# A six-stage decoder kernel: loads of a group split by reader, and the last norms written to the second state buffer

## The reference

```
x = LN(x + retention(x))               # 8 heads of 16, decay mask, group norm, gate
x = LN(x + cross_attention(ctx, x))    # 8 heads of 16, masked softmax over 64 context tokens
x = LN(x + moe(x))                     # 8 experts, top 2, rerouted by a similarity matrix
x = LN(x + attention(x))               # 16 heads of 64, scores outside a band of 129 set to 0
x = LN(x + attention_with_context(x))  # 16 heads of 8, 64 context tokens put before the 64 own
x = LN(x + block(x))                   # rotary attention, LN, 8 experts of 512 (gelu), top 2, LN
```

## Time and profile before

| | us |
|---|---|
| median of the runs | 2297.73 |
| the profiled execution | 2298.89 |
| its span | 2297.3 |
| PE busy (85%) | 1944.6 |
| DVE busy (54%) | 1234.6 |
| ACT busy (38%) | 875.9 |
| POOL busy (16%) | 376.7 |
| PE idle until the last of the six loads landed | 44.5, at 8 places |
| PE idle until a reloaded `X` landed | 15.6, at 3 places |

### The profile page before, as it was taken

How to read it: one execution, slowest core, us unless ns; L and a number is a source line. 1 busy time by engine, 2 the same in 40 slices (tenths; PEclk the granted TensorE clock), 3 DMA queues, 4 the chain that set the end, 5 groups by cost and what they waited for, 6 DMA issues and landing times.

```text
span 2297.3 us, 41641 instructions
## 1 busy us (share of the span) xinstructions
PE 1944.6 (85%) x17716; PEld 1380.0 (60%) x17716; DVE 1234.6 (54%) x3227; ACT 875.9 (38%) x1472; POOL 376.7 (16%) x370
## 2 busy tenths in 40 slices
PE   4867767678888899988898998988989989888996
PEld 3645555554556676655666665565766655566764
DVE  5657565647556533466656235656643457565331
ACT  1212122112456353335554433355443333553532
POOL 5132322300201101012111011111011021011011
PEclk8777777769899799999988999999889999997999
DMA  4010101010000012100000121000002210000121
GB/s 168 6 51 1 56 1 56 1 37 1 11 1 11 1 38 65 47 19 11 11 1 1 56 65 45 3 11 11 2 19 61 59 29 11 1 11 1 38 61 41
DMA packets 82201, 64.21 MB, mean 28 GB/s; under 512 B 15960, under 2 KB 69216, under 8 KB 81760
## 3 DMA queue, kind: packets, MB, share of 16 engines
q1 hardware_dynamic: 82016, 61.56, 9.0%
HBM read 57.35 MB, written 4.19 MB: 27 GB/s over the span
## 4 chain that ended last, share of the span: by engine, by line
PE 60%; DVE 21%; ACT 7%; POOL 6%; issue 3%; DMA 2%; SPq 1%; POOLq 0%; DVEq 0%
PE bank L1636 10%; PE bank L1627 9%; PE bank L1413 4%; DVE P L1080 4%; DVE gs L1079 4%; PE bank L1525 4%; PE bank L1250 3%; PE bank L1588 3%; PE bank L1421 3%; DVE X L893 2%; PE bank L1493 2%; PE bank L1438 2%; PE bank L1576 2%; PE bank L1265 2%; PE bank L1536 2%
## 5 line engine op out<-in xcount | busy, mean ns | idle before, releaser
L1068 DVE SCALAR_TENSOR_TENSOR R<-bank,gs,R 128x128 f32<-128x128 f32 x480 | 134.5, 343 | 297.2 <-PE bank L1636 251.8
L861 ACT ACTIVATE PT<-bank,cols 128x512 f32<-128x512 f32 x256 | 174.4, 686 | 298.1 <-PE bank L1627 297.7
L1636 PEld LDWEIGHTS bank<-w2r,PT 128*128 128x128 f32 x2048 | 236.3, 192 | 49.3 <-ACT PT L861 39.9
L1636 PE MATMUL bank<-w2r,PT 128*128 128x128 f32 x2048 | 246.1, 277 | 21.7 <-ACT PT L861 21.7
L763 ACT ACTIVATE P<-P 128x512 f32<-128x512 f32 x256 | 159.2, 629 | 250.5 <-DVE P L1080 249.1
L1627 PE MATMUL bank<-XT,w1r 128*128 128x512 f32 x512 | 242.5, 609 | 3.1 <-DVE R L1209 3.1
L1079 DVE TENSOR_REDUCE gs<-bank 128x8 f32<-128x512 f32 (+1 forms) x256 | 174.5, 682 | 96.1 <-PE bank L1525 66.3
L1250 PE MATMUL bank<-const,P 128*128 128x128 f32 x1152 | 181.8, 298 | 33.1 <-POOL P L652 14.5
L1250 PEld LDWEIGHTS bank<-const,P 128*128 128x128 f32 x1152 | 143.9, 152 | 93.8 <-ACT P L763 36.8
L594 POOL TENSOR_SCALAR rstd<-mv 128x4 f32<-128x4 f32 x64 | 14.7, 230 | 1126.8 <-DVE mv L885 1126.8
L1080 DVE TENSOR_TENSOR P<-bank,gs 128x512 f32<-128x512 f32 x256 | 176.9, 691 | 8.8
(11 more groups left out here) (205 smaller groups left out, 3245.0 us busy)
## 6 DMA issues: line engine op xcount, KB each, us to landing
w1r<-in_w SPq DMA_DIRECT2D x64, 256.0 KB, 2.7
w2r<-in_w SPq DMA_DIRECT2D x64, 256.0 KB, 3.1
wb<-in_wb SPq DMA_DIRECT2D x1, 4228.0 KB, 17.4
V<-in_ctxT SPq DMA_DIRECT2D x16, 256.0 KB, 3.7
XT<-in_xT SPq DMA_DIRECT2D x8, 256.0 KB, 2.9
X<-in_x SPq DMA_DIRECT2D x8, 256.0 KB, 4.1
V<-in_mask SPq DMA_DIRECT2D x8, 256.0 KB, 4.2
x_mid<-X SPq DMA_DIRECT2D x8, 256.0 KB, 2.3
```

The lines of the kernel that those rows point to most:

```text
L861: act.activation(PT[s][:, c, :], banks[s][c % 3][:, :], ACT.Gelu, bias=Col("b1", NC * e + c)).then_inc(b_gelu.of(s), 1)
L1068: last = dve.scalar_tensor_tensor(R[s][:, t, :], bank[:, 128 * t:128 * t + 128], share[s][:, t, e:e + 1], src[:, t, :], ALU.mult, ALU.add)
L1636: ins = mm(tile(banks[s][3], t), tile(PT[s][:, c, :], t), w2r[e % 2][:, c, :], start=c == 0, stop=c == NC - 1)
```

## The change

The six loads of a group are split into three parts with a semaphore each: `XT` (`xT_loaded`, PE waits at `qk`), context and masks (`ctx_loaded`, waited for at `kv` by PE and at `qk.3` by POOL), and `X` (`x_loaded`, waited for by DVE at `o`). Each is issued for the slot's next group when its buffer has had its last reader in this one: context and masks after `q`, `X` after its transpose and POOL's copy with the bias, `XT` after the gate logits. PE's `qk` now also waits for `a_g_done` of the slot's group before.

The last norm of each phase is written to `X1` in place of `X`, and stored from there. So the load of the next `X` needs no wait for a store; in phase 2 it is issued as soon as POOL 687 has read `X` (`b_r2`). POOL waits for the store before it writes `X1` again, much later in the next group. At the start of the program `X` is loaded after the masks. Many signals of phase 2 now go on counting on a semaphore of phase 1, which adds no instruction.

All tables in `ORDERS` but `pool1` have new numbers.

```diff
 ORDERS = dict(
-    sp1=(0, 1, 1, 1, 2, 1, 3, 1, 4, 1, 5, 1, 6, 1, 7, 1),
+    sp1=(0, 2, 1, 2, 0, 2, 1, 2, 2, 2, 3, 2, 2, 2, 3, 2, 4, 2, 5, 2, 4, 2, 5, 2, 6, 1, 7, 1),
...
-    pe2=(0, 1, 1, 1, 0, 1, 1, 1, 0, 1, 1, 1, 0, 1, 1, 1, 0, 2, 1, 2, 0, 1, 1, 1, 0, 3, 1, 3, 0, 3, 1, 3, 0, 3, 1, 3,
...
             def second(n, s, last):
+                if not last:
+                    yield "q"
+
+                    sp.wait_ge(a_q.of(s), a_q.at(n, s))
+                    load_context(n + 1, s)
+                    yield "o2"
+                    sp.wait_ge(a_x_ps.of(s), a_x_ps.at(n, s, use=0))
+                    sp.wait_ge(a_x_bias.of(s), a_x_bias.at(n, s))
+                    load_x(n + 1, s)
+                    yield "g"
+                    sp.wait_ge(a_g_ps.of(s), a_g_ps.at(n, s))
+                    load_xT(n + 1, s)
                 yield "gb"
                 sp.wait_ge(a_x.of(s), a_x.at(n, s, use=1))
-                apart(sp)
-                sp.dma_start(token_rows(x_mid, n, s), X[s][:, :, :]).then_inc(stored[s], 16)
-                if not last:
-
-                    sp.wait_ge(a_g_done.of(s), a_g_done.at(n, s))
-                    apart(sp)
-                    sp.wait_ge(stored[s], 16 * n + 16)
-                    apart(sp)
-                    loads(n + 1, s)
+                sp.dma_start(token_rows(x_mid, n, s), X1[s][:, :, :]).then_inc(stored[s], 16)
...
+                if not last:
+                    yield "n5s"
+
+                    sp.wait_ge(b_r2.of(s), b_r2.at(n, s))
+                    load_state(n + 1, s)
                 yield "n5"
                 sp.wait_ge(b_x.of(s), b_x.at(n, s, use=3))
-                apart(sp)
-                sp.dma_start(token_rows(out, n, s), X[s][:, :, :]).then_inc(written[s], 16)
-                if not last:
-                    sp.wait_ge(written[s], 16 * n + 16)
-                    apart(sp)
-                    load_state(n + 1, s)
+                sp.dma_start(token_rows(out, n, s), X1[s][:, :, :]).then_inc(written[s], 16)
...
                 yield "on"
-                norm_apply(n, s, a_ln_rstd, a_x, 1)
+                norm_apply(n, s, a_ln_rstd, a_x, 1, X1[s])
...
                 yield "n5"
-                norm_apply(n, s, b_ln_rstd, b_x, 5)
+                norm_apply(n, s, b_ln_rstd, b_x, 5, X1[s])
...
-                pe.wait_ge(loaded[s], 16 * 6 * (n + 1))
+                if n:
+                    pe.wait_ge(a_g_done.of(s), a_g_done.at(n - 1, s))
+                pe.wait_ge(xT_loaded[s], 16 * (n + 1))
...
                 yield "kv"
                 pe.wait_ge(a_x.of(s), a_x.at(n, s))
+                pe.wait_ge(ctx_loaded[s], 16 * 4 * (n + 1))
```

More of the change, by code:

```diff
@@ L82, in then @@
     def then(self, passes, each=1, uses=1):
-        assert len(self.sems) == SLOTS
-        return Signal(self.sems, each, uses, self.at(passes - 1, 0, use=self.uses - 1))
+        return Signal(self.sems, each, uses, self.at(passes - 1, SLOTS - 1, use=self.uses - 1))
 class Steps:
@@ L333, in build @@
         s_const2 = sem("s_const2")
-        loaded = [sem(f"loaded{s}") for s in range(SLOTS)]
+        xT_loaded = [sem(f"xT_loaded{s}") for s in range(SLOTS)]
+        x_loaded = [sem(f"x_loaded{s}") for s in range(SLOTS)]
+        ctx_loaded = [sem(f"ctx_loaded{s}") for s in range(SLOTS)]
         stored = [sem(f"stored{s}") for s in range(SLOTS)]
-        a_qk_ps = signal("a_qk_ps", 4)
-        a_qk_mul = signal("a_qk_mul", 4)
+        a_qk_ps = signal("qk_ps", 4)
+        a_qk_mul = signal("qk_mul", 4)
         a_k_sum = signal("a_k_sum", 3)
@@ L342, in build @@
         a_v_diag = signal("a_v_diag")
-        a_tanh = signal("a_tanh")
+        a_tanh = signal("tanh")
         a_gated = signal("a_gated")
@@ L356, in build @@
         a_hT = signal("a_hT")
-        a_o_ps = signal("a_o_ps")
+        a_o_ps = own("o_ps", 1, 2)
         a_ln_mv = own("ln_mv", 1, 2)
@@ L372, in build @@
         a_pT = own("pT", 4)
-        a_r_ps = signal("a_r_ps", 4)
-        a_r = signal("a_r")
+        a_r_ps = own("r_ps", 4)
+        a_r = own("r")
         a_rt_ps = own("rt_ps")
         a_rT = own("rT")
-        a_o2_ps = signal("a_o2_ps")
-        a_g_ps = signal("a_g_ps")
+        a_g_ps = signal("g_ps")
         a_g_diff = own("g_diff", 1)
         a_g_exp = own("g_exp", 1)
-        a_g_done = signal("a_g_done")
+        a_g_done = signal("g_done")
         a_x_bias = own("x_bias", 1)
-        a_spread = signal("a_spread")
+        a_spread = signal("spread")
         dve1, pool1 = Steps(sem("dve1")), Steps(sem("pool1"))
@@ L420, in build @@
         b_up_ps = own("b_up_ps", 2, 8)
-        b_tanh = own("b_tanh", 1, 8)
+        b_tanh = a_tanh.then(passes, 1, 8)
         b_fh = own("b_fh", 1, 8)
@@ L447, in build @@
         b_pT = a_pT.then(passes, 4, 8)
-        b_r_ps = own("b_r_ps", 1, 6)
-        b_r = own("b_r", 1, 6)
+        b_r_ps = a_r_ps.then(passes, 1, 6)
+        b_r = a_r.then(passes, 1, 6)
         b_rt_ps = a_rt_ps.then(passes, 1, 2)
         b_rT = a_rT.then(passes, 1, 2)
-        b_o_ps = own("b_o_ps", 1, 2)
-        b_fqk_ps = signal("b_fqk_ps", 4)
-        b_frot = signal("b_frot", 4)
+        b_o_ps = a_o_ps.then(passes, 1, 2)
+        b_fqk_ps = a_qk_ps.then(passes, 4, 1)
+        b_frot = a_qk_mul.then(passes, 4, 1)
         b_fsum = signal("b_fsum", 2)
@@ L459, in build @@
         b_fv = signal("b_fv")
-        b_g_ps = signal("b_g_ps")
+        b_g_ps = a_g_ps.then(passes)
         b_g_diff = a_g_diff.then(passes)
         b_g_exp = a_g_exp.then(passes)
-        b_g_done = signal("b_g_done")
+        b_g_done = a_g_done.then(passes)
         b_b2_ps = signal("b_b2_ps")
@@ L466, in build @@
         b_x_bias = a_x_bias.then(passes, 1, 3)
-        b_spread = signal("b_spread")
+        b_spread = a_spread.then(passes)
         b_tspread = signal("b_tspread", 1, 4)
@@ L490, in token_rows, with load_xT, load_x, load_context @@
                 return dram[bass.ds((n * SLOTS + s) * NT, NT), :].rearrange("(t p) d -> p t d", p=128)
-            def loads(n, s):
+            def load_xT(n, s):
                 t0 = (n * SLOTS + s) * NT
-                sp.dma_start(XT[s][:, :], d["xT"][:, bass.ds(t0, NT)]).then_inc(loaded[s], 16)
+                sp.dma_start(XT[s][:, :], d["xT"][:, bass.ds(t0, NT)]).then_inc(xT_loaded[s], 16)
+            def load_x(n, s):
+                sp.dma_start(X[s][:, :, :], token_rows(d["x"], n, s)).then_inc(x_loaded[s], 16)
+            def load_context(n, s):
+                t0 = (n * SLOTS + s) * NT
                 for c in range(2):
                     sp.dma_start(ctxT[s][:, c, :], d["ctxT"][c * 128:c * 128 + 128, bass.ds(t0, NT)])\
-                      .then_inc(loaded[s], 16)
-                sp.dma_start(X[s][:, :, :], token_rows(d["x"], n, s)).then_inc(loaded[s], 16)
+                      .then_inc(ctx_loaded[s], 16)
                 sp.dma_start(maskr[s], d["mask"][bass.ds(t0, NT)].partition_broadcast(128))\
-                  .then_inc(loaded[s], 16)
+                  .then_inc(ctx_loaded[s], 16)
                 sp.dma_start(maskc[s][:, :], d["mask"][bass.ds(t0, NT)].rearrange("(t p) -> p t", p=128),
-                             allow_slow_non_contiguous=True).then_inc(loaded[s], 16)
+                             allow_slow_non_contiguous=True).then_inc(ctx_loaded[s], 16)
+            def loads(n, s):
+                load_xT(n, s)
+                load_context(n, s)
+                load_x(n, s)
             def first(n, s):
@@ L627, in second @@
                 yield "q"
+                if n:
+                    pool.wait_ge(stored[s], 16 * n)
                 with_bias(n, s, a_x, a_x_bias, "xbo")
@@ L645, in first2 @@
                 yield "aq0"
+                if n:
+                    pool.wait_ge(written[s], 16 * n)
                 with_bias(n, s, b_x, b_x_bias, "abo", 0)
@@ L979, in first @@
                 dve.wait_ge(a_o_ps.of(s), a_o_ps.at(n, s))
+                dve.wait_ge(x_loaded[s], 16 * (n + 1))
                 st1(dve.tensor_tensor(R[s][:, :, :], tok(banks[s][2][:, :]), X[s][:, :, :], ALU.add))
@@ L1024, in second @@
                 yield "o2"
[L1025 removed]
+                dve.wait_ge(a_o_ps.of(s), a_o_ps.at(n, s, use=1))
                 dve.wait_ge(a_x_bias.of(s), a_x_bias.at(n, s))
@@ L1360, in second @@
                     ins = mm(o, tile(OT[s], t), tile(A("xo"), 1), start=False, stop=True)
-                ins.then_inc(a_o2_ps.of(s), 1)
+                ins.then_inc(a_o_ps.of(s), 1)
                 yield "x"
                 pe.wait_ge(a_x.of(s), a_x.at(n, s, use=1))
-                turn_state(s, 3, X, a_x_ps)
+                turn_state(s, 3, X1, a_x_ps)
                 yield "g"
```

23 lines of the change are left out of this document (14 added, 9 removed), and 176 rows, old and new, of tables (act1, act2, dve1, dve2).

## The result

The changed kernel takes 2177.18 us, median of 4 runs (2176.25 to 2178.56); the kernel before, run beside it, 2292.18. The ratio is 0.950, 95% interval 0.944 to 0.956. The profiled execution took 2176.25 us with a span of 2174.5. The one of before had 2297.3, so the span fell by 122.8 us. The medians differ by 115.0, since the execution profiled before (2298.89) was 6.7 us above the median.

What follows compares the result with a forecast made beforehand. It took phase 1 to be bound by chains from engine to engine and phase 2 nearly by PE. Its terms summed to 61.5 us less than the profiled 2298.89, forecast 2237 us, range 2202 to 2276.

Steps and rivals of the forecast that it cites:

- The clock: PE's granted clock around phase 1's `qk` stalls: claimed the stall alone didn't lower it, so nothing was counted.
- Rival 1: Clock comes back in phase 1's six `qk`, 19 us less than forecast: 2218 us; chance 13%.
- The six stalls and the start: PE's waits for loads at `qk` in phase 1 go, -28.5 us; waits at program start shorten, -5 us.
- Rival 2: Phase 1 stays bound by its chains, the time returns in other waits, none of 28.5 gained: 2265.5 us; chance 15%.
- Softmax order of phase 1: Slot 1's score tiles come ahead of slot 0's products on PE, so DVE idles less: 2 us four times, -8.
- The reload: Phase 2's reload of `X` for slot 1 is issued earlier, with PE work placed there: 3 x 5.2, -15.6 us.
- Rival 3: Phase 2 gives nothing at its seams: reload idle turns into waits for POOL, start is even: 2260.6 us; chance 15%.
- The start of phase 2: Slot 1's experts fill PE's idle time in layer 4; slot 0's seven alone lose 3 us: -8 us taken.
- `fv`: PE's waits for values of layer 6's attention, 22.3 us at eight places, covered by the other slot's stages: -18 us.
- `cs` behind `cr`: PE's waits for DVE's output tile come at three places a pass, not one: 8 more at 2.7, +21.6 us.
- rival 5: Slower through POOL's scaled tiles in phase 2, 89.5 us more waiting: 2326 us; decides from 4.75 us a round; chance 5%.

Runs made afterwards that it cites:

- E5: Kernel before, with three unread extra products on PE ahead of `qk`'s wait for the six loads, groups 2 to 7: 2268.40 us, ratio 0.993.
- E1: Changed kernel with all engines' order tables taken from the kernel before, keeping the new loads: 2248.96 us, ratio 0.981.
- E9: Changed kernel with slot 0's first scores of layer 6 moved back directly behind its `fv` on PE, all four passes: 2205.16 us, ratio 0.965.
- E3: Changed kernel with phase 2's order tables taken from the kernel before; loads and phase 1 stay new: 2222.83 us, ratio 0.969.

## Why the prediction was wrong, by its own steps

1. **The clock** is the step that failed. "So the stall alone didn't bring it down, and my sum leaves the clock as it is": the first half holds, the second does not follow. I asked what had lowered the clock and not what kept it low. Busy time fell by 48.7 us, of which the six stalls are 20 (E5: 19.4; E1: 21.7). Rival 1 had that mechanism and I gave it 13%. Its 19 us agree with these 20 partly by luck: it had all six `qk` at 6.40 us falling to 3.2, but they gave 11.4 in the kernel after (36.9 to 25.5 us) and 14.7 in E5, and the rest came behind them. It was also too narrow, since busy time fell in other places too: 7.9 us more with phase 1's orders, and 19.1, give or take 10, in phase 2. The Trainium skill's rule, "TensorE: Matmul & The Clock Gate", section "Why this matters for your kernels", that idle gaps between bursts of matmuls make the throughput drop in mid-kernel, is borne out by E9, where the clock falls from 1.00 behind a wait of 3.9 us. E5 shows something else that a gap does: the clock was low ahead of it, and filling it brought the clock back. I had set the rule aside on one row.
2. *The six stalls and the start*, 33.5: right in sum, 32.6 of idle time (E1). `qk` began at 8.10 rather than 13.09, and what it waits for there is POOL's memset, not `XT`. The second wait at the start did not go, as I had said it would: slot 1's `qk` waited 4.16 us for its `XT` (2.87 before). Rival 2 fell. A pass of phase 1 takes 99 us where I said 107: the 12 us of idle time came as forecast (35.2 to 23.3), and 8.4 of busy time (84.1 to 75.7) came on top.
3. *Softmax order of phase 1*, 8: all of phase 1's new orders together give 9.1 of idle time, and 7.9 of busy time that I had not counted. DVE's waits for score tiles fell from 4.1 us a pass to 0.5; no run takes these apart from the rest.
4. *The reload*, 15.6: right in mechanism; the loads alone give nothing in the passes (E3), the order makes them count. Rival 3 therefore fell only because both were changed.
5. *The start of phase 2*, 8: wrong, though the time seems to fit. From the first `sh` to the first store of the output it takes 397.83 us after and 405.46 in E3, 7.6 less. But only 3.3 of these are idle time (46.9 to 43.6), the rest is clock, and PE's waits for `fv`'s values, 5.5 us of that idle time, belong to the next term. So nothing is left for the start. The loss was mis-sized: slot 0's experts alone wait 1.27 us seven times (8.9 where I had 3). My chain of 3.05 us from product to `down` was nearly right (438.15 to 441.31, 3.16), but I set PE's `down` of 1.05 against it, and that stands ahead of the chain, not in it. So an expert takes 4.15 us from `down` to `down`.

```profile
437.16 1.16 PE L1443 MATMUL bank<-wb,P 128*128 128x128 f32 x8 [1.27 <-DVE P L1116]
438.15 1.88 PE L1435 MATMUL bank<-XT,wb 128*128 128x512 f32 x4
441.31 1.16 PE L1443 MATMUL bank<-wb,P 128*128 128x128 f32 x8 [1.27 <-DVE P L1116]
```

6. *`fv`*, 18: 22.3 of waiting, the whole. E9 shows 29 us for 15.4 of it.
7. *`cs` behind `cr`*, +21.6: wrong. The waits for DVE rose by 6.3 (10.7 to 17.0), to 3.0 once and 0.7 twice a pass. That DVE has less queued at the two others may be the reason; no run tells it. `cs`'s waits for ACT fell from 10.2 to 3.4 at the same time, so in sum it cost nothing. I had multiplied the largest wait by the count.
8. Not in the sum: PE's waits for the norms from DVE, 19.6 before and 5.9 now, against 2.1 and 8.5 for POOL's copies of them, and 5.6 new at `sh`.

The idle time alone fell by 74.1 where I had 61.5. Phase 1's part was right (41.7, and 41.5 in my sum), phase 2's too small (32.4 and 20.0), where `cs` cost nothing and the start gave nothing. The high end of my range has a slip: rival 2 without the softmax part is 2265.5 + 8 = 2273.5, not 2276. No rival on the other side came near: POOL's tiles wait 15.1, or 0.9 a round, far below the 4.75 from which rival 5 decides.

## What to carry to other kernels

Price a wait on the matmul engine twice: once its length, once what the work behind it takes at the lower clock against the higher. Here 74.1 us of idle time taken out of PE came with 115.0 us in the medians, 1.55 us for each, but the second price is not a constant: loads alone gave 21.7 us of busy time for 32.6 of idle time in one order and 10.4 for 47.9 in another. A low clock ahead of a gap is no sign that the gap is free: ask where the clock would be if the work went on, and test it by filling the gap with products that nobody reads. Then look at the whole pass, and not only at the work right behind the gap: such a fill gave 19 us at six stalls in the kernel before. Ahead of `kv` in the kernel after it gave nothing, because the clock that came back there was lost again at the scores.

## What the runs showed of the hardware

The clock fell while PE was fully busy. In a pass of phase 1 of the kernel after it is at 1.00 until about 290.8, where the first set of 128 products of 64x17 ends, and at 0.50 from 291 to 294, with PE busy for all of the us from 291 to 292. It is back at 1.00 from 295, falls again as the second set ends at 301.14 (0.59 from 301.0 to 301.5), and from 302.6 to 309 stays at 0.50 through `o2`, with PE busy for 6.38 of 6.40 us. The two sets in PE's timeline:

```profile
286.79 3.91 PE L1369 MATMUL bank<-Q,PT 64*64 64x17 f32 x128
...
297.23 3.91 PE L1369 MATMUL bank<-Q,PT 64*64 64x17 f32 x128
```

That these small products are the cause is argued from their place only; no run tells it. Behind the second set PE also waits 0.56 us. What is also open is why the clock comes back sooner at some places than at others: 2.5 us into `qk` after, but only at its end before.
